# Wide attention with its scores turned, projection parts stored as they are made, and the first head operands on two queues

## The reference

```python
x = x + tanh(g_xattn[0]) * _L0_xattn_ref(ctx, ctx, layernorm(x), ...)   # 16 heads of 16
x = x + tanh(g_ffn[0])   * _L0_ffn_ref(layernorm(x), ...)               # 4 experts, the best one
x = x + tanh(g_xattn[1]) * _L1_xattn_ref(layernorm(x), ctx, ctx, ...)   # one head of 256
x = x + tanh(g_ffn[1])   * _L1_ffn_ref(layernorm(x), ...)               # product-key memory

# _L1_xattn_ref, "wide attention"
scores = einsum('bqe,bke->bqk', Q, K) / sqrt(256)      # 512 x 1601 per batch
attn = softmax(scores, axis=-1)
out = einsum('bqk,bke->bqe', attn, V);  return einsum('bse,fe->bsf', out, O_weight)
```

## Time and profile before

| | us |
|---|---|
| median of 3 runs (3539.31 to 3543.54) | 3540.04 |
| the profiled execution | 3540.9 |
| its span, first to last instruction | 3539.2 |
| TensorE busy in the span | 3340.9 (94%) |
| VectorE, ScalarE, GpSimd busy | 2440.0, 1550.5, 322.3 |

### The profile page before, as it was taken

The page is one execution under the profiler, slowest core; times in us unless marked ns, Lnnn a source line. Parts: engine busy times, 40 slices in busy tenths (PEclk is TensorE's granted clock), DMA queues, the critical chain, the costliest instruction groups (busy, mean ns, idle before and its releaser), DMA issues. The chain is left out here.

```text
span 3539.2 us, 61791 instructions
## 1 busy us (share of the span) xinstructions
PE 3340.9 (94%) x21900; PEld 1996.7 (56%) x21900; DVE 2440.0 (69%) x5488; ACT 1550.5 (44%) x2750; POOL 322.3 (9%) x449
## 2 busy tenths in 40 slices
PE   9979999999999999779959999969999999999999
PEld 5643222222222222668834554438888989898988
DVE  5538888989898885610023444349888888888886
ACT  5534888888888888112212222212222222222221
POOL 0023111111111110210010000000000000000000
PEclk9987999999999999789979999989999999999999
DMA  6687676757576640421111131130000000000000
GB/s 244 232 257 100 100 105 102 103 99 110 96 106 100 90 75 6 176 101 36 36 40 49 55 104 55 49 138 9 12 10 12 10 12 10 12 10 12 9 12 8
DMA packets 148227, 256.67 MB, mean 73 GB/s; under 512 B 23848, under 2 KB 99472, under 8 KB 147536
## 3 DMA queue, kind: packets, MB, share of 16 engines
q1 hardware_dynamic: 133136, 218.83, 29.2%
q0 software_dynamic: 10288, 31.21, 2.7%
q10 hardware_dynamic: 4624, 4.46, 0.4%
HBM read 170.38 MB, written 83.64 MB: 72 GB/s over the span
## 5 line engine op out<-in xcount | busy, mean ns | idle before, releaser
L697 DVE TENSOR_REDUCE at_pmax<-at_psm 128x2 f32<-128x1024 f32 (+1 forms) x832 | 944.8, 1179 | 126.9 <-PE at_psm L528 122.2
L634 ACT ACTIVATE ring<-at_pss 128x512 f32<-128x512 f32 (+1 forms) x1664 | 895.1, 595 | 194.6 <-PE at_pss L552 191.4
L552 PE MATMUL at_pss<-at_qs,at_ks 99*128 99x512 bf16 (+1 forms) x1664 | 512.6, 387 | 8.9 <-ACT ring L634 7.1
L1730 PE MATMUL mt_psd<-mt_xl,mt_key_in 128*128 128x128 f32 x4096 | 491.0, 278 | 2.2 <-DMA mt_key_out<-m_out 2.2
L1730 PEld LDWEIGHTS mt_psd<-mt_xl,mt_key_in 128*128 128x128 f32 x4096 | 469.6, 193 | 3.6 <-DMA mt_key_out<-m_out 2.3
L1756 PE MATMUL mt_psu<-mt_key_out,mt_g 128*128 128x256 f32 x2048 | 447.4, 379 | 1.3 <-DVE mt_g L1966 1.3
L560 PE MATMUL at_pso<-ring,at_vw 128*32 128x512 f32 (+1 forms) x3328 | 444.1, 606 | 0.0
L1756 PEld LDWEIGHTS mt_psu<-mt_key_out,mt_g 128*128 128x128 f32 x2048 | 386.7, 190 | 52.6 <-DVE mt_g L1966 1.4
L552 PEld LDWEIGHTS at_pss<-at_qs,at_ks 99*128 99x128 bf16 (+1 forms) x1664 | 116.5, 98 | 484.2 <-ACT ring L634 427.8
L1818 ACT ACTIVATE mt_g<-mt_psd 128x512 f32<-128x512 f32 x256 | 152.9, 598 | 351.0 <-PE mt_psd L1730 350.7
L526 PE MATMUL at_psm<-at_ks,at_qs 64*128 64x512 bf16 (+1 forms) x1024 | 272.3, 344 | 14.2 <-DVE at_pmax L697 9.7
(11 more groups left out here) (224 smaller groups left out, 3933.3 us busy)
## 6 DMA issues: line engine op xcount, KB each, us to landing
at_ks<-k_dram SPq DMA_DIRECT2D x192, 200.1 KB, 6.5
k_dram<-pj_kp SPq DMA_DIRECT2D x24, 800.5 KB, 5.5
xs_dram<-at_qf POOLq DMA_DIRECT2D x68, 256.0 KB, 3.0
v_dram<-pj_v SPq DMA_DIRECT2D x8, 1664.0 KB, 9.1
at_vd<-v_dram SPq DMA_DIRECT2D x32, 416.0 KB, 10.4
at_kh<-k_dram SPq DMA_DIRECT2D x128, 100.1 KB, 5.5
wide_ctxT<-ctxT SPq DMA_DIRECT2D x8, 1601.0 KB, 7.2
at_qs<-q_dram SPq DMA_DIRECT2D x192, 64.0 KB, 6.7
```

The source lines that it names most:

```text
L552: nc.tensor.matmul(ps_s[0:r, score_slot(u, n), :], ks[:, g, j, kt * P:kt * P + r], qs[:, g, j, :], start=True, stop=True).then_inc(s_mm, 1)
L634: nc.scalar.activation(pr[0:r, (NST * g + n) % PRING, :], ps_s[0:r, score_slot(u, n), :], ACT.Exp, scale=SCALE).then_inc(expd, 1)
L697: nc.vector.tensor_reduce(heads, found, AX.X, ALU.max).then_inc(m_red, 1)
L1730: ins = nc.tensor.matmul(ps_d[:, j % 2, y * P:y * P + P], key_in[:, k, j * YB + y, :], xl[:, s, k, :], start=k == 0, stop=k == KC - 1)
```

## The change

Three parts. *Projections:* K's parts are stored as soon as its eight chunks are through, V when it is out, then the context is loaded, and Q's parts are stored last. *Start of the heads:* for head group 0 of batch 0 the loads of `kh`/`qh` are issued by ScalarE, those of the first four pairs of parts count on another semaphore, and the maximum products wait for these 16 alone, the scores for the rest; each maximum product stands ahead of its key product, and the first two of head group 1 ahead of the remaining key products. *Wide attention:* the scores are made with the keys on the partitions, tile by tile in a ring of four PSUM banks, and ScalarE copies each tile to SBUF (`sT`). VectorE keeps a running maximum over the tiles (`keep_max`, 12 per batch). TensorE transposes the result (`turn_top`), VectorE reduces it to a peak per token and multiplies it into the rows of an identity (`find_peaks`), and a product with ones spreads the peaks over all partitions (`spread_rows`). VectorE subtracts them (`shift`, 13 per batch), ScalarE takes the exponential in place. GpSimd adds up the 13 tiles (`add_probs`, 12 additions), and TensorE sums over partitions with four products of one column (`sums`). The context product (`u_tile`) reads `sT` directly; the transposes of probabilities and their copies are gone. Each engine's order is written out anew without loops, with `sT`, `gT` and the context rows in two buffers:

```diff
 # project, SP
                 def step(i, s, load):
                     b = i * PB + s
-                    sp.wait_ge(third, (b + 1) * NCH)
...
+                    sp.wait_ge(third, b * NCH + NKC)
+                    parts_out("k")
                     sp.wait_ge(v_out, (b + 1) * KT + 2)
...
                     if load:
 
                         sp.wait_ge(v_mm, (b + 1) * KT)
                         sp.dma_start(ctx[:, s, :, :], t["ctxT_in"][b + PB]).then_inc(ctx_in[s], 16)
+                    sp.wait_ge(third, (b + 1) * NCH)
+                    parts_out("q")
 # attend_heads
+        def operands_in(g, n, used):
+
+            return t["consts"] if not used and g == 0 and n < MAX_PARTS else kq_in[g]
...
+                    for n in range(len(Q_PART)):
+                        low_in(sp, b, g, n, used)
+                        if n < MAX_PARTS and (used or g > 0):
+                            high_in(sp, b, g, n, used)
...
                 for n in range(NJ):
-                    key_product(n)
                     max_product(0, 0, 0, n)
-                for n in range(NJ, MH * len(halves)):
                     key_product(n)
                 for n in range(MBANKS):
                     max_product(0, 1, 1, n)
+                for n in range(NJ, MH * len(halves)):
+                    key_product(n)
                 pe.wait_ge(k_out, len(halves))
                 turn_max(0)
...
+                for n in range(MAX_PARTS):
+                    high_in(act, 0, 0, n, False)
 # attend_wide, TensorE
+    NORMS_AT, OUT_AT, MIX_AT, LAST_AT = 4, 1, 7, 9
+    ROWS_AT, TOTAL_AT = (4, 9), 6
...
+                def score_tile(b, kt):
+
+                    r = key_rows(kt)
+                    if kt >= RING:
+                        pe.wait_ge(s_out, b * KT + kt - RING + 1)
+                    elif kt == RING - 1:
+                        pe.wait_ge(shifted, b * KT)
+                    elif b:
+                        pe.wait_ge(s_out, b * KT)
+                    for k in range(KC):
+                        ins = nc.tensor.matmul(ps_s[0:r, slot(b, kt), :], ctxT[:, b % 2, k, kt * P:kt * P + r], gT[:, b % 2, k, :],
                                                start=k == 0, stop=k == KC - 1)
                     ins.then_inc(s_mm, 1)
...
+                def turn_top(b):
+
+                    pe.wait_ge(s_max, (b + 1) * (KT - 1))
+                    pe.wait_ge(xnT_out, min(b + 2, B))
...
+                def sums(b):
+
+                    pe.wait_ge(summed, (b + 1) * (KT - 1))
+                    for q in range(QT):
+                        ins = nc.tensor.matmul(ps_p[:, 1, 0, q:q + 1], total[:, q * P:q * P + P], ones[:, 0:1], start=True, stop=True)
+                    ins.then_inc(peaks_mm, 1)
...
+                for b in range(B):
+                    pe.wait_ge(gT_out, b + 1)
+                    pe.wait_ge(ctxT_in[b % 2], (b // 2) * 16 + 16)
+                    for kt in range(KT):
+                        score_tile(b, kt)
+                        if kt == OUT_AT and b >= 2:
+                            out_product(b - 2)
+                        if kt == NORMS_AT and b + 1 < B:
+                            turn_norms(b + 1)
+                        if kt == MIX_AT and b + 1 < B:
+                            a_product(b + 1)
+                        if kt == LAST_AT and b >= 3:
+                            pe.wait_ge(xnT_out, min(b + 2, B))
+                            turn_last(b - 3)
+                    if b == 0:
+                        turn_top(0)
+                        spread_rows(0)
+                        continue
+                    u_ready(b - 1)
+                    for kt in range(KT):
+                        u_tile(b - 1, 0, kt)
+                        if kt == ROWS_AT[0]:
+                            turn_top(b)
+                        elif kt == ROWS_AT[1]:
+                            spread_rows(b)
+                    for kt in range(KT):
+                        ins = u_tile(b - 1, 1, kt)
+                        if kt == TOTAL_AT:
+                            sums(b - 1)
+                    ins.then_inc(u_mm, 1)
 # ScalarE
+                for b in range(B):
...
+                    for kt in range(KT):
+                        r = key_rows(kt)
+                        act.wait_ge(s_mm, b * KT + kt + 1)
+                        nc.scalar.activation(sT[0:r, s, kt, :], ps_s[0:r, slot(b, kt), :], ACT.Copy).then_inc(s_out, 1)
...
+                    for kt in range(KT):
+                        r = key_rows(kt)
+                        act.wait_ge(shifted, b * KT + kt + 1)
+                        nc.scalar.activation(sT[0:r, s, kt, :], sT[0:r, s, kt, :], ACT.Exp, scale=SCALE).then_inc(expd, 1)
+                    if b + 2 < B:
+                        root(nth["next", b + 2])
+                    if b >= 2:
+                        root(nth["last", b - 2])
+                    if b:
+                        copy(uT[:, :, :], u_at[b - 1], u_mm, b, uT_out)
 # VectorE
+                for b in range(B):
+                    for kt in range(1, KT):
+                        keep_max(b, kt)
+                        if kt == OUT_AT + 2 and b >= 2:
+                            add_out(b - 2)
+                    if b >= 3:
+                        last_stats(b - 3)
+                    find_peaks(b)
+                    dve.wait_ge(peaks_mm, max_rows(b))
+                    for kt in range(KT):
+                        shift(b, kt)
+                    if b:
+                        invert(b - 1)
+                    if b + 2 < B:
+                        norms(b + 2)
+                    if b >= 2:
+                        last_norms(b - 2)
 # GpSimd
+                    pool.wait_ge(expd, b * KT + kt + 1)
+                    if kt == 1:
+                        if b:
+                            pool.wait_ge(peaks_mm, sums_mm(b - 1))
+                        before = sT[0:r, b % 2, 0, :]
+                    else:
+                        pool.wait_ge(summed, b * (KT - 1) + kt - 1)
+                        before = total[0:r, :]
+                    nc.gpsimd.tensor_tensor(total[0:r, :], before, sT[0:r, b % 2, kt, :], ALU.add).then_inc(summed, 1)
```

More of the change, by code:

```diff
@@ L1207, in attend_wide @@
     SCALE = 1.0 / float(D) ** 0.5
-    GR = [(a, min(4, KT - a)) for a in range(0, KT, 4)]
-    NG = len(GR)
+    RING = 4
+    NORMS_AT, OUT_AT, MIX_AT, LAST_AT = 4, 1, 7, 9
+    ROWS_AT, TOTAL_AT = (4, 9), 6
+    order = [("next", 0), ("next", 1)]
+    for b in range(B):
+        order += [("next", b + 2)] * (b + 2 < B) + [("last", b - 2)] * (b >= 2)
+    order += [("last", B - 2), ("last", B - 1)]
+    nth = {job: n + 1 for n, job in enumerate(order)}
     with Stage(nc, "aw") as st:
-        ctxT, ctx = t["wide_ctxT"], t["wide_ctx"]
+        ctxT, ctx = t["wide_ctxT"], (t["wide_ctx"], st.sb("ctx1", [P, KT, D]))
@@ L1287, in turn_norms @@
                 def turn_norms(b):
-                    pe.wait_ge(normed, (b + 1) * QT)
+                    pe.wait_ge(normed, nth["next", b] * QT)
                     for k in range(KC):
@@ new lines, in turn_top, with spread_rows @@
+                def turn_top(b):
+                    pe.wait_ge(s_max, (b + 1) * (KT - 1))
+                    pe.wait_ge(xnT_out, min(b + 2, B))
+                    if b >= 3:
+                        pe.wait_ge(l_out, b - 2)
+                    for q in range(QT):
+                        ins = nc.tensor.transpose(ps_p[:, 0, q, :], top[:, q * P:q * P + P], t["ident"][:, :])
+                    ins.then_inc(peaks_mm, 1)
+                def spread_rows(b):
+                    pe.wait_ge(peaked, b + 1)
+                    pe.wait_ge(s_out, b * KT + KT - RING + 1)
+                    nc.tensor.matmul(ps_s[:, slot(b, KT), :], ones[:, :], rows[:, :, :].rearrange("p q n -> p (q n)"),
+                                     start=True, stop=True).then_inc(peaks_mm, 1)
@@ new lines, in _ @@
+                u_ready(B - 1)
+                pe.wait_ge(s_out, B * KT)
+                pe.wait_ge(shifted, B * KT)
+                for m in range(KC):
+                    for kt in range(KT):
+                        ins = u_tile(B - 1, m, kt)
+                        if m == 0 and kt == ROWS_AT[0]:
+                            out_product(B - 2)
+                            pe.wait_ge(peaked, B)
+                            turn_last(B - 3)
+                        elif m == 1 and kt == ROWS_AT[0]:
+                            pe.wait_ge(l_out, B - 2)
+                            sums(B - 1)
@@ L1391, in _ @@
+                ins.then_inc(u_mm, 1)
+                pe.wait_ge(normed, nth["last", B - 2] * QT)
+                turn_last(B - 2)
                 pe.wait_ge(o_out, B - 1)
-                for m in range(KC):
-                    ins = u_product(1, m, range(KT))
-                ins.then_inc(u_mm, 1)
-                turn_last(B - 2)
                 out_product(B - 1)
@@ L1448, in _ @@
+                last_out(B - 3)
```

(5 more changed lines are left out.)

352 lines of the change are left out of this document (151 added, 201 removed).

## The result

The changed kernel takes 3489.6 us (median of 4 runs, 3488.6 to 3490.6); the kernel before, on the same chip, takes 3541.7 (4 runs, 3539.3 to 3543.5). The ratio is 0.985, with a 95% interval of 0.9837 to 0.9862. So the change brings some 52 us where 86 were forecast, and the time lies outside the range given. The profiled execution spans 3488.9 us, 50.3 less than that of before.

A forecast was written before the change was run, and what follows sets the result against it. TensorE was taken to bound wide attention. Its stretch falls from 531.0 to 456.4 us, 73.6 less with the gather; with 9.5 from projections and 3.1 from heads, 86.2 less than 3540.9, 0.9 over the median: 3454, range 3440 to 3482.

The forecast's parts named there:

- Bound and work: Wide attention: TensorE stays the bound, with 434.5 us of work; no other engine bounds a batch of 55 us.
- The first two batches and their clock: Wide attention, batches 0 and 1: waits of 10.1 us without a context product as cover, plus 3 for lower clock.
- The wait before the output product: Wide attention, batches 2 to 5: TensorE waits 2.2 us each for ScalarE's copy of the context result, 8.8 in all.
- The third rival, "slower than before": Wide attention: new waits lower the granted clock after every batch's out product; 3560 at a mean of 0.80, chance 0.04.
- VectorE and GpSimd take turns at SBUF: Wide attention: GpSimd's additions beside the first norms delay VectorE; 3477 at chance 0.15 or 3457 at chance 0.2.
- wide case: Wide attention: residual sum and four normalizations each wait up to 1.27, 6.4 us in four batches; 3477, chance 0.15.
- narrow case: Wide attention: only VectorE instructions with two SBUF inputs wait, 2.8 instead of 2.2 in four batches; 3457, chance 0.2.
- Projections: End of projections: storing K and V earlier leaves only Q's parts at the end, a gain of 9.5 us.
- Heads: Start of the heads: first maximum 4.5 us earlier, first scores, hanging on the transpose, 3.1 earlier.
- Gather and tail: Context-row loads beside GpSimd's first token gather cost 1 us; the part behind wide attention stays the same.
- a period over 60: Wide attention, sign of a wrong forecast; 56 to 58 us between mixing products would show it right.

The follow-up runs named there:

- copy first: Changed kernel with ScalarE's copy of uT put ahead of the square root of the last norm: 3449.0 us, ratio 0.9735 to the kernel before.
- both edits: Changed kernel with GpSimd's additions after the last normalization and ScalarE's uT copy ahead of the square root: 3447.9 us, ratio 0.9736 to the kernel before.
- adds later: Changed kernel with GpSimd starting a batch's additions only after VectorE's last normalization of that round: 3451.3 us, ratio 0.9741 to the kernel before.

## Why the prediction was wrong, step by step

- **Bound and work (right).** By the forecast's terms a batch without waits is 55.5 us of TensorE's work, and with the copy first the period is 55.5. TensorE stayed the bound, and neither the transposed maximum nor the sums made it wait in the steady batches.
- **The first two batches and their clock (right in sum, partly by luck).** With the waits before the output product gone, the wide stretch takes 445.7 us (both edits) and 448.9 (copy first); the forecast without its 8.8 for that wait is 447.6. The members are off in both directions. The idle time is 6.6 us with both edits and 9.8 with the copy first, for a forecast of 10.1: the fifth score tile waits 1.0 to 2.3 instead of 3.3, and the 3.05 for the normalizations of batch 2 were not in the list. TensorE's busy time is 439.1 in both, 4.6 above the 434.5 of work, where the forecast had 3 for the clock.
- **The wait before the output product (the step that failed).** "A wait of 1.5. If VectorE's first sum of norms has to stand out one addition of GpSimd (1.27), it is 2.8 ... I take 0.7, the middle, thus 2.2". The bound was set for one instruction, when the chain ahead of the copy holds eight that may have to wait out an addition: L1584, the residual sum, the four first normalizations and the variances of both norms. Beside the additions L1584 costs 0.95 more, the residual sum nothing (it came first), the normalizations 3.85, the variances 0.17 and 0.65. On top of the 0.62 without any collision that makes 6.24, and the wait was 6.27. That is 16.3 us over four batches. The base of 1.5 was too high: with no collision (adds later) it is 0.6.
- **The clock behind it (not in the forecast at all).** The four output products took 24.6 us instead of 14.5, 10.1 more. Stretches of the changed kernel around the product at 2016.61:

```profile
2010.00:2014.00 4.00, 0.33 (x1) 0.00 (x0) 4.00 (x6) 0.00 (x0) 3.69 (x3) 1.00 0.87 296
2014.00:2017.00 3.00, 0.39 (x1) 0.39 (x2) 2.51 (x9) 1.56 (x4) 2.60 (x3) 0.61 0.00 0
2017.00:2020.00 3.00, 3.00 (x8) 2.37 (x8) 3.00 (x4) 0.53 (x2) 2.70 (x3) 0.50 0.02 5
2020.00:2023.00 3.00, 3.00 (x10) 2.28 (x10) 0.68 (x2) 0.00 (x0) 2.39 (x3) 0.75 0.26 70
```

  TensorE is idle for 6.3 us, and the granted clock goes from 1.00 to 0.50 (2.4 to 1.2 GHz) late in the wait; the product then runs at the low level. The third rival, "slower than before", named this place, the output product, for the wrong price: it put the fall over all the work, when the product loses 2.1 to 2.8 us after each long wait and the score tiles behind it are back at their usual time.
- **The rival that happened.** "VectorE and GpSimd take turns at SBUF", wide case, 3477 at a chance of 0.15: "the residual sum and the four normalizations each stand out up to 1.27, 6.4 us". The mechanism was right and its size nearly so; add the 10.1 of the clock and it gives 3487. I held it at 0.15 because GpSimd is busy 17 of 57 us. But the average says nothing of place: the additions and the norms are both released by the end of the same sums product, so from the second batch on they coincide every time. (In the same rival the narrow case gives 3456 by its own terms, not 3457.)
- **The Trainium skill's rule, read by half.** For the narrow case I cited the Trainium skill, SBUF — State Buffer, section "Who interferes with whom", for instructions with two SBUF inputs alone. The same section also says that `tensor_scalar`, which the normalizations are, can enter a mode that takes the pair of ports shared with GpSimd, and that the loser stands still until the other's instruction is over. The traces agree with both halves: 1140 ns for `tensor_scalar`, against 410 to 420 alone, 1176 ns for the form with two inputs (no run has it alone), 0.9 to 1.6 us instead of 0.69 for the running maximum, and a 128x4 `tensor_scalar` that takes 1065 beside an addition of 1267.
- **Projections (right):** 9.5 forecast, 10.6 in the trace, the wait of TensorE 7.12 instead of 17.67.
- **Heads (wrong in what is late next).** The first maximum product starts without a DMA wait, as forecast. But the forecast said "the first scores hang on that transpose", and in the changed kernel they hang on the transfer of the maxima's rows, which SP issues behind the loads of three head groups: 9.0 earlier than before, when the projections alone bring 10.6. By the end of the heads 0.9 of the start is lost, where 3.1 more was forecast. This trace is a late one (62.1 us after the first load, 60.1 on average over eight), so part of the loss is scatter; on average the gain is 0.4, from one trace of the kernel before.
- **Gather and tail:** ahead of the first mixing product 1.9 us are lost (1 forecast), and the part behind wide attention, forecast at nothing, lost 3.2.

The sum: 86.2 forecast, less 16.3 (wait) and 10.1 (clock), 1.8 for the rest of the wide stretch, 4.0 for the heads, 3.2 behind and 1 ahead, plus 1.1 from the projections, leaves 50.9; the spans differ by 50.3, and 0.6 stays unassigned. The 1.8 are 2.0 more of low clock in the first two batches less 0.2 of waits there. Of what the prediction named as signs, a period over 60 stood for wrong, and it is 64.5.

## What to carry to other kernels

When two engines are given work that one and the same event releases, compare them instruction by instruction from that event on; a busy share of 30% hid a full collision here. Then look for what stands behind the delayed chain on a third engine's queue: here one copy, moved ahead of a square root it had nothing to do with, was worth 40 us of 3490 and left 3 us of the collision's price. And price a wait of TensorE together with the instructions behind it, which may run at half the clock: here 6.3 us of wait brought 2.1 to 2.8 us more.

## What was new about the hardware

- In these traces VectorE's instructions with two SBUF inputs, its `tensor_scalar` from SBUF to SBUF and GpSimd's additions exclude each other by whole instructions, in both directions: a 128x4 `tensor_scalar` waited out an addition (1.18 us instead of 0.23), and an addition waited out a residual sum (2.33 instead of 1.26). Additions set the pace of the normalizations, one per 1.41 us, and did not become longer by them.
- Not touched by the additions were the statistics (one SBUF input: 411 to 415 ns in every kernel) and the output sum, whose other input is in PSUM: with the adds later it ran in the midst of the additions (1.65 us for four) in the same time as in the changed kernel, where the additions are over by then. The Trainium skill, same page and section, says that an instruction with at most one SBUF input outside those modes does not contend; these two rows agree.
- Waits of TensorE of 0.6, 1.4 and 1.6 us left the output product at 3.72 us, waits of 6.3 made it 5.7 to 6.5.
- The transfers of the maxima's rows, three of 4 KB, took 2.5 to 7.9 us to land (medians of the three) in eight traces with the same code ahead of them, loads of three head groups, and the scores' wait for them was anything from 0.4 to 9.1 us. In the one trace with two groups ahead they took 1.8.
